# Bias and softmax branch summed in PSUM: two products of 256 columns ahead of an output projection

## What is computed

```python
xn = layernorm(x)
# cosine attention: power-16 scores, then a projection with a bias
cosine = einsum('bto,po->btp', cosine_heads(xn), Wo) + bo
# softmax attention, no projection; mixture of 8 experts, top 2
softmax_out = softmax(q @ k.T / sqrt(8)) @ v
moe_out = sum_e combine[e] * (xn @ W_experts[e] + b_experts[e])
x = x + cosine + softmax_out + moe_out
# layer 2: layernorm(x), causal attention, fp4-quantised gated FFN
```

## Time and profile before

| | |
|---|---|
| median of 3 runs | 1978.48 us (1976.43 to 1978.59) |
| profiled execution, its own time | 1968.91 us |
| span in that profile | 1967.1 us |
| mean granted TensorE clock in it | 0.856 of full speed |
| instructions | 38505 |

### The profile page before, as it was taken

One profiled execution on the slowest core, in us unless ns is written; L12 is line 12 of the kernel. 1 busy time (PEld: TensorE's weight loads), 2 busy tenths in 40 slices (PEclk: granted clock), 3 DMA queues, 4 the chain that ended last, 5 costly groups with the idle time before them and its releaser, 6 DMA issues.

```text
span 1967.1 us, 38505 instructions
## 1 busy us (share of the span) xinstructions
PE 1475.6 (75%) x12022; PEld 751.1 (38%) x12022; DVE 1761.1 (90%) x3977; ACT 1778.4 (90%) x1888; POOL 1183.2 (60%) x540
## 2 busy tenths in 40 slices
PE   2677778777778777777878777778778778777765
PEld 1223434333443433344343334434334434333333
DVE  5779998999999999999999999999999999999864
ACT  1299999999999999999999999999999999999993
POOL 1556666666666666666666656665666666665640
PEclk9667898889888988988898888898888888888876
DMA  1000000000000000000000000000000000000000
GB/s 42 3 4 1 6 1 6 5 6 6 6 5 0 6 5 6 6 6 5 0 6 5 6 6 6 0 6 6 5 6 5 6 0 6 6 5 6 4 3 6
DMA packets 21058, 11.19 MB, mean 6 GB/s; under 512 B 1431, under 2 KB 20953, under 8 KB 20956
## 3 DMA queue, kind: packets, MB, share of 16 engines
q1 hardware_dynamic: 20956, 10.20, 1.8%
HBM read 6.00 MB, written 4.19 MB: 5 GB/s over the span
## 4 chain that ended last, share of the span: by engine, by line
DVE 37%; issue 22%; ACT 20%; PE 18%; DVEq 2%; SPq 0%; POOL 0%; ACTq 0%; DMA 0%; POOLq 0%
ACT curve L578 10%; DVE nmax L885 6%; DVE curve L875 5%; ACT root L578 4%; PE psM L1045 4%; DVE curve L879 3%; PE psM L1037 3%; DVE acc L859 3%; DVE xn L781 1%; PE psS L1095 1%; DVE h L454 1%; PE psM L1207 1%; PE psM L1190 1%; DVE stkT L871 1%; ACT prob L578 1%
## 5 line engine op out<-in xcount | busy, mean ns | idle before, releaser
L530 POOL TENSOR_TENSOR root<-curve 128x2048 f32<-128x2048 f32 x128 | 478.9, 3741 | 453.2 <-DVE curve L879 453.2
L578 ACT ACTIVATE curve<-curve 128x2048 f32<-128x2048 f32 x384 | 719.1, 1907 | 5.6 <-POOL curve L533 2.2
L578 ACT ACTIVATE root<-root 128x2048 f32<-128x2048 f32 x256 | 484.7, 1906 | 0.0
L533 POOL TENSOR_TENSOR curve<-curve,root 128x2048 f32<-128x2048 f32 x64 | 354.6, 5562 | 65.2 <-ACT root L578 65.2
L879 DVE TENSOR_SCALAR curve<-psS 128x1024 f32<-128x1024 f32 x256 | 308.2, 1215 | 2.7 <-PE psS L1068 1.9
L885 DVE TENSOR_REDUCE nmax<-psS 128x4 f32<-128x1024 f32 x256 | 302.7, 1213 | 0.9 <-PE psS L1077 0.9
L578 ACT ACTIVATE prob<-psS 128x1024 f32<-128x1024 f32 x256 | 256.6, 1029 | 32.8 <-PE psS L1097 31.1
L566 POOL TENSOR_TENSOR stk<-qk,stk 128x512 f16<-128x512 f32 x128 | 148.1, 1167 | 73.4 <-ACT stk L578 72.9
L1045 PE MATMUL psM<-we,xnT 128*128 128x512 f32 x256 | 172.4, 762 | 0.0
L875 DVE TENSOR_TENSOR curve<-curve,root 128x2048 f32<-128x2048 f32 x64 | 161.0, 2516 | 6.1 <-ACT root L578 6.1
L1077 PE MATMUL psS<-stkT 32*128 32x256 f16 x1024 | 103.1, 294 | 80.7 <-DVE curve L879 42.5
(11 more groups left out here) (194 smaller groups left out, 2818.0 us busy)
## 6 DMA issues: line engine op xcount, KB each, us to landing
xt<-in_L_attn_x SPq DMA_DIRECT2D x32, 128.0 KB, 2.2
out<-yo SPq DMA_DIRECT2D x32, 128.0 KB, 1.8
we<-in_L_ffn_W_experts SPq DMA_DIRECT2D x1, 512.0 KB
curve<-in_L_attn_w_qkv SPq DMA_DIRECT2D x1, 192.0 KB
curve<-in_L_ffn_w_down SPq DMA_DIRECT2D x1, 176.0 KB
curve<-in_L_ffn_w_gate SPq DMA_DIRECT2D x2, 64.0 KB
curve<-in_L_ffn_w_up SPq DMA_DIRECT2D x2, 64.0 KB
curve<-in_L_ffn_W_qkv SPq DMA_DIRECT2D x1, 128.0 KB
```

The lines of the kernel that those rows point to most:

```text
L530: nc.gpsimd.tensor_tensor(root[:, two], curve[:, p, two], curve[:, p, two], ALU.mult).then_inc(s_sq, 1)
L533: nc.gpsimd.tensor_tensor(curve[:, p, two], curve[:, p, two], root[:, two], ALU.mult).then_inc(s_half[0], 1)
L578: return nc.scalar.activation(out, in_, func, **kw)
```

## The change

POOL loses its stages residual and fadd. The bias bo and the softmax branch `of` enter the sum on PE instead: in the stage wo, ahead of the wait for ocT, one product of a row of ones with the bias row (borow, bo twice side by side, 256 columns) opens the accumulation in the bank, and a second product of the identity with `of` (256 columns) adds to it; the two projection products then accumulate on top. Ahead of the two, PE waits for finf, which is when `of` is there. The experts' first two instructions read x instead of acc. The waits follow: DVE's experts wait for x and for x1 of two batches earlier in place of POOL's residual, DVE's wo waits for the experts in place of fadd, and DVE's finf waits for the projection product of the batch before. In the start-up bob goes (a product and a copy), bo is loaded by two transfers in place of one, and the row of ones has a buffer of its own.

```diff
     "gpsimd": [
-        ("fadd", 0, -1), ("sq", 2, 0), ("sq", 3, 0), ("norm", 0, 1), ...
-        ("unit", 0, 1), ("stack", 2, 1), ("stack", 3, 1), ("residual", 0, 1), ("mul", 0, 0), ...
+        ("sq", 2, 0), ("sq", 3, 0), ("norm", 0, 1), ...
+        ("unit", 0, 1), ("stack", 2, 1), ("stack", 3, 1), ("mul", 0, 0), ...
...
-        bob = sb("bob", [P, D])
+        borow = sb("borow", [1, NT * D])
+        onerow = sb("onerow", [1, P])
...
-            sp.dma_start(brow[:, 3 * D + E:], bo.rearrange("(a n) -> a n", a=1)).then_inc(s_w, 16)
+            for j in range(NT):
+                sp.dma_start(borow[:, j * D:(j + 1) * D], bo.rearrange("(a n) -> a n", a=1)).then_inc(s_w, 16)
...
-                if stage == "residual":
-                    pool.wait_ge(s_x[p], due(s_x[p], b, LANDED[p]))
-                    pool.wait_ge(s_x1, due(s_x1, b - 2))
-                    nc.gpsimd.tensor_tensor(acc[:, p, :, :], xt[:, p, :, :], bc(bob[:, :], 1, NT), ALU.add).then_inc(s_acc0, 1)
...
-                if stage == "fadd":
-                    pool.wait_ge(s_finf, due(s_finf, b))
-                    pool.wait_ge(s_moe, due(s_moe, b))
-                    nc.gpsimd.tensor_tensor(acc[:, p, :, :], acc[:, p, :, :], of[:, :, :], ALU.add).then_inc(s_acc2, 1)
...
                 if stage == "experts":
-                    dve.wait_ge(s_acc0, due(s_acc0, b))
+                    dve.wait_ge(s_x[p], due(s_x[p], b, LANDED[p]))
+                    dve.wait_ge(s_x1, due(s_x1, b - 2))
...
+                        so_far = xt if e == 0 else acc
...
                 if stage == "finf":
-                    dve.wait_ge(s_acc2, due(s_acc2, b - 1))
+                    dve.wait_ge(s_wop, due(s_wop, b - 1))
...
                 if stage == "wo":
                     bank, k = misc_bank(stage, 0, 0)
                     dve.wait_ge(s_wop, due(s_wop, b))
-                    dve.wait_ge(s_acc2, due(s_acc2, b))
+                    dve.wait_ge(s_moe, due(s_moe, b))
...
                     pe.wait_ge(last, value)
+                    pe.wait_ge(s_finf, due(s_finf, b))
+                    mm(bank[:, 0:T], onerow[:, :], borow[:, :], start=True, stop=False)
+                    mm(bank[:, 0:T], ident[:, :], of[:, :, :].rearrange("p j d -> p (j d)"), start=False, stop=False)
                     pe.wait_ge(s_ocT, due(s_ocT, b))
                     for j in range(NT):
-                        ins = mm(bank[:, j * D:(j + 1) * D], ocT[:, j * P:(j + 1) * P], woT[:, :], start=True, stop=True)
+                        ins = mm(bank[:, j * D:(j + 1) * D], ocT[:, j * P:(j + 1) * P], woT[:, :], start=False,
+                                 stop=(j == NT - 1))
                     ins.then_inc(s_wop, 1)
```

More of the change, by code:

```diff
@@ L79 @@
         ("m", 3, 1), ("m", 4, 1), ("mul", 1, 0), ("c", 0, 1), ("hmul", 0, -1), ("m", 5, 1), ("m", 6, 1),
-        ("mul", 3, 0), ("hmul", 1, -1), ("choose", 4, 1), ("quanth", 0, -1), ("c", 1, 1),
-        ("m", 7, 1), ("down", 0, -2),
+        ("mul", 3, 0), ("hmul", 1, -1), ("choose", 4, 1), ("quanth", 0, -1), ("c", 1, 1), ("m", 7, 1),
+        ("down", 0, -2),
     ],
@@ L93 @@
     "gpsimd": [
-        ("fadd", 0, -1), ("sq", 2, 0), ("sq", 3, 0), ("norm", 0, 1), ("high", 0, 1), ("high", 1, 1), ("stack", 0, 1),
-        ("stack", 1, 1), ("unit", 0, 1), ("stack", 2, 1), ("stack", 3, 1), ("residual", 0, 1), ("mul", 0, 0),
-        ("mul", 2, 0), ("sq", 0, 1), ("sq", 1, 1),
+        ("sq", 2, 0), ("sq", 3, 0), ("norm", 0, 1), ("high", 0, 1), ("high", 1, 1), ("stack", 0, 1), ("stack", 1, 1),
+        ("unit", 0, 1), ("stack", 2, 1), ("stack", 3, 1), ("mul", 0, 0), ("mul", 2, 0), ("sq", 0, 1), ("sq", 1, 1),
     ],
@@ L247, in build @@
         yo = sb("yo", [P, 2, NT, D])
-        ones1 = yo[0:1, 0, 0, :]
         spare = curve[:, 1, :]
@@ L254, in build @@
         wfl = spare[:, 52 * D:54 * D]
-        brow = spare[0:1, 32 * D:32 * D + 4 * D + E]
+        brow = spare[0:1, 32 * D:32 * D + 3 * D + E]
         bload = spare[0:3, 40 * D:40 * D + E * D]
@@ L279, in build @@
         s_lnst, s_lnact, s_lnnr, s_xn = sem("ln0_stats", 3), sem("ln0_rstd_guess", 2), sem("ln0_newton", 3), sem("xn_ready", 2)
-        s_acc0 = sem("residual_ready", 1)
         s_xnTp, s_xnT = sem("xnT_in_psum", 1), sem("xnT_ready", 1)
@@ L300, in build @@
         s_wln, s_pow = sem("score_ln", 4), sem("power16_ready", 4)
-        s_finfp, s_finf, s_acc2 = sem("softmax_out_in_psum", 1), sem("softmax_out_chain", 2), sem("softmax_out_added", 1)
+        s_finfp, s_finf = sem("softmax_out_in_psum", 1), sem("softmax_out_chain", 2)
         s_fincp, s_finc = sem("cosine_out_in_psum", 1), sem("cosine_out_chain", 3)
@@ L402, in build @@
         TRANSPOSES += [(wdq[:, c * P:c * P + CH[c]], wdT[0:CH[c], c, :]) for c in range(NCH)]
-        BIAS_ROWS = [(brow[0:1, 0:3 * D + E], wfb[:, :]), (brow[0:1, 3 * D + E:], bob[:, :])]
+        BIAS_ROWS = [(brow[0:1, :], wfb[:, :])]
         PRODUCTS = [(wload[:, 4, :], wload[:, 5, :], wqk1[:, :]), (wload[:, 6, :], wout1T[:, :], wvo1[:, :])]
         SETUP_USES = len(TRANSPOSES) + len(BIAS_ROWS) + len(PRODUCTS)
-        WEIGHT_DMAS = 4 + 2 + 2 * NCH + 1 + 4 + 3 + 3
+        WEIGHT_DMAS = 4 + 2 + 2 * NCH + 1 + 4 + 3 + 2 + NT
         block = ctx.enter_context(nc.Block())
@@ L508, in _ @@
             link(nc.gpsimd.memset(best[:, :, :], -1.0))
-            link(nc.gpsimd.memset(ones1, 1.0))
+            link(nc.gpsimd.memset(onerow[:, :], 1.0))
             link(nc.gpsimd.memset(unity[:, :], 1.0))
@@ L858, in run @@
                             dve.wait_ge(s_moe, due(s_moe, b, 8 * arg + n + 1 - NT))
+                        so_far = xt if e == 0 else acc
                         nc.vector.scalar_tensor_tensor(acc[:, p, j, :], bank[:, (e % 4) * D:(e % 4 + 1) * D],
-                                                       comb[:, p, j, e:e + 1], acc[:, p, j, :], ALU.mult,
+                                                       comb[:, p, j, e:e + 1], so_far[:, p, j, :], ALU.mult,
                                                        ALU.add).then_inc(s_moe, 1)
@@ L1014, in _ @@
                 else:
-                    mm(bank, ones1, src, start=True, stop=True).then_inc(s_wps, 1)
+                    mm(bank, onerow[:, :], src, start=True, stop=True).then_inc(s_wps, 1)
             pe.wait_ge(s_wcp, SETUP_USES)
```

## The result

The changed kernel takes 2016.29 us, the median of five executions (2014.19 to 2029.71), against 1977.52 us for the kernel before, measured beside it. By the medians it is 38.8 us slower; the ratio of all executions is 1.0219, with 1.0196 to 1.0242 as its 95% interval. The direction of the prediction holds, and the time lies in its range, 1978 to 2020 us. Its number, 1996 us, does not hold: 38.8 us stand against the forecast 17.6 us, and that the range still has the time is luck, since its upper end came from the half case.

A forecast was written before the change was run, and what follows sets the result against it. It took DVE, ACT and PE as one chain through the output projection, so delay there lengthens the tick: 24 x 0.6 + 8 x 1.2 - 8 x 0.84 = 17.3, plus 0.3 start-up; 1978.5 + 17.6 = 1996 us, range 1978 to 2020.

The forecast's parts named there:

- the half case: Rival: the output projection stage stays at half clock, +35 to +52 us, 2013 to 2030 us; chance 0.13.
- the price at the full clock: Two added 256-column products on PE ahead of the projection: 1.06 us together at 2.4 GHz.
- full stage: Oc to lnv with the projection at 2.4 GHz: 3.84 us before, forecast 0.6 us longer (0.5 to 0.75).
- the reserves: Slack in the full-clock tick: at most 0.14 us ahead of the projection, 0.10 ahead of x1, 0.2 taken ahead of lnv.
- the new waits: PE's wait for finf is met early; DVE's experts wait once more in two stages, at most 2.6 us, taken as 0.
- a quarter of the ticks as half: Forecast mix at the output projection: 8 of 32 ticks at half clock, 24 at full, against 16 and 16 before.
- half stage: Oc to lnv with the projection at 1.2 GHz: 4.68 us before, forecast 1.2 us longer, the clock recovering behind the products.
- the rest of the tick: From lnv to the next oc: 53.14 and 53.47 us in two ticks, taken as unchanged by the edit.
- signs of being right: In the profile after: x1 waits for PE in nearly every tick, 0.5 us and more; oc to lnv 4.4 us or longer.
- Small terms: PE's earlier finf wait and DVE's extra expert waits at 0, one more start-up transfer at 0.3 us.
- POOL's adds gone: POOL loses two adds a tick that nobody waited for: worth 0, with 0.02 us a tick as end of range.
- faster, by the clock: Rival: PE's extra work keeps the full clock in the rest of the tick too, -13.4 us, 1965 us; chance 0.06.

The follow-up runs named there:

- e12: Changed kernel plus four unused products of constants in PE's gaps: two ahead of its wait for oc, one ahead of p1T, one ahead of pvw 3; 1975.72 us.
- e1: Kernel before plus two products of constants ahead of the wait for ocT, overwritten by the projection; POOL keeps its adds; 2016.67 us, ratio 1.0208.
- e2: Changed kernel without the two products and the wait for finf, so bias and softmax branch are left out; 1966.65 us, ratio 0.9947.
- e8: Changed kernel plus two unused products of constants on PE, one ahead of p1T and one ahead of pvw 3; 2003.08 us, ratio 1.0121.
- a1: The changed kernel run again unedited, for a second profile; 2013.95 us, ratio 1.0180 to the kernel before.
- e13: Kernel before plus four unused products of constants: two ahead of PE's wait for oc, one ahead of p1T, one ahead of pvw 3; 1944.59 us, ratio 0.9839.
- e9: Changed kernel with bias and softmax products moved ahead of PE's wait for oc, plus unused products ahead of p1T and pvw 3; 1941.38 us, ratio 0.9814.
- e5: Kernel before plus two unused products of constants in PE's gap ahead of its wait for oc; 1976.17 us, ratio 0.9999.
- e7: The whole change, with bias and softmax products moved into PE's gap ahead of its wait for oc; 1957.92 us, ratio 0.9930.
- e4: Kernel before with only the softmax branch moved to PE by one product and fadd dropped; the bias stays on POOL; 1979.33 us, ratio 1.0030.
- e3: Kernel before plus two unused DVE multiplies of constants right behind x1; 2031.36 us, ratio 1.0275.
- e6: Kernel before plus two DVE reductions of constants right behind x1, no work added on PE; 1973.62 us, ratio 0.9995.
- e11: Kernel before plus three DVE reductions of constants behind x1, no work added on PE; 1981.48 us, ratio 1.0023.
- e10: Kernel before plus two unused products of constants on PE, one ahead of p1T and one ahead of pvw 3; 1969.79 us, ratio 0.9951.

## Why the prediction was right and wrong

**Right: the price at the full clock, and what pays for it.** 1.06 us for the two products, 0.6 us a full stage after the reserves: 1.06 and 0.65 us in the tick shown, 0.63 to 0.67 us in e12's 20 full stages. Of the reserves only the 0.2 us ahead of lnv showed: counted from oc, the projection starts 0.88 us later than in the full tick of before, x1 0.86 us and lnv 0.65 us. The two products stand behind e 3 and ahead of the projection, nothing there hides them, and x1 waits in 31 ticks. That the adds of POOL and the new waits bring no part of the loss is shown by e1 and e2.

**Wrong: the mix, "a quarter of the ticks as half".** One stage of 26 was wholly full. The argument was made from the length of the ticks and a PE that is fuller in the stage. What the rows show instead is that the clock falls in 25 of 26 stages, 1.8 to 2.6 us behind the start of oc: during the second product in the tick of 1109.98, from the projection on in that of 1051.39. A fall at that time did no harm in before, since the projection was nearly through; now the projection stands in it. The half stage with the clock low from 0.5 us on, the only one that the prediction knew, came in none of the 26 ticks. Nor did a stage with a low clock behave as priced. I let the clock come back behind the products; it fell there. The stage of 5.41 us is 0.73 us longer than the half one of before, where 1.2 had been priced, and 1.57 us longer than the full one. By the prediction's mix the mean stage would have grown by 0.54 us a tick; it grew by 0.85, which is 10 us more in 32 ticks.

**Wrong: "the rest of the tick" unchanged.** In the profiled execution this is the larger miss, 31.7 of 53.8 us. I had compared the rest after a full and after a half stage in one trace, found 53.14 and 53.47 us, and taken it as fixed for a stage of any make. Two ticks could not carry that: in before the rest goes from 52.69 to 55.19 us behind stages of the same 3.85 us. The rest grew by 1.22 us a tick, since the low clock moved from where DVE and ACT cover it to the qkv products, 2.2 us each time, in 13 of 26 ticks. e8 removes this part, with the rest back at 53.47 us, and 13 us are gained by the medians; without slow qkv it still loses 26.9 us, so in the timed executions the stage is likely the larger part. The prediction had asked only what a longer stage does to the clock at the stage, and never which other part of the tick would get the slow stretch instead; its signs of being right (x1 waits in nearly every tick, oc to lnv of 4.4 us and more) came true and could not show it. The windows of the four quarters of before would have shown where there was something to lose: in the fourth it stood at 0.99.

**Small terms.** POOL's adds gone: 0 forecast, 9 us gained without the products (e2), nothing seen beside them (e1 and a1, e13 and e9). The rival "faster, by the clock" had 0.06. It named the right lever, but not the place: e5 and e7 show that columns ahead of the transposes of oc hold the stage at the full clock, and e9 what that is worth when the other gaps are filled too. With the gap ahead of oc filled, 26 of 26 stages are full in e5, e7, e9 and e13 and 20 in e12, where 7 were in before and 1 in after. The Trainium skill (TensorE: Matmul & The Clock Gate, A second HAM failure mode) says that a PE which idles briefly and often between its groups of matmuls is throttled again and again; by that, filling such gaps pays, and e9, e12 and e13 agree, with gaps of 0.7 to 2 us. The equal gaps in two ticks, one with fast and one with slow qkv, say that the gap at hand isn't the whole condition.

**Open.** Why the low clock moves into the qkv products when columns are added around the output projection (after, a1, e1, e4, e5 and e7: 4 to 14 ticks), and hardly when DVE is delayed instead (e3, e6 and e11: 3, 1 and 0). What goes with it in the waits is that PE stands still ahead of p1's transposes in 27 to 30 ticks of the first group, in 22 to 24 of the second and in 16 of before; what makes that decide is not settled. Nor is it shown what e2 gains by, nor how the 38.8 us of the timed executions divide, since only the profiled ones have a trace.

## What to carry to other kernels

Price work for PE by the place as much as by its columns: the same two products cost 40 us behind a gap and on the path (e1), nothing in the gap (e5), and gained 25 us there once PE's other two gaps were filled (e13 against e10). Before pricing, cut a tick into quarters and read the granted clock beside the busy time of the other engines: where the clock is full and another engine waits for PE is where a moved slow stretch can cost, even if the edit is nowhere near. And compare the mean clock of the two runs: where it is unchanged and the time is not, look for what moved.

## What I had not expected of the hardware

Unused products made the kernel faster: e13 is the kernel before plus four products a tick that nobody reads, and it takes 1944.59 us, 1.6% less. The mean granted clock of the profiled executions rose from 0.856 to 0.879 (0.885 in e9). The mean alone does not tell the time, though: e12 has 0.878 and takes 31 us longer than e13 with 0.879.

An added product isn't charged in proportion: one costs 4 us (e4), two cost 39 (after). At the full clock the stage grows by 0.24 and 0.65 us; what goes with the remainder is the clock, by the counts in the table: 14 against 1 full stages, 5 against 13 slow qkv.

DVE's multiply of two operands in SBUF took 1.11 to 1.53 us beside POOL's stack products and 0.55 to 0.57 us without (e3); its reduction of one operand took 0.53 to 0.55 us in both cases (e6). The clip, whose source is in PSUM, takes the same with and without POOL's adds (1215 and 1216 ns).
